# Picking 36 of 128 columns with a selection matrix, in place of a full transpose, behind the rotary attention

## The chip, the cores and the metric

The kernel runs on one core of a Trainium2 chip. The metric is the device time in microseconds (us), as the median of three runs. A core has five engines that run at the same time and wait for each other through semaphores: TensorE (PE; its weight loads are shown apart as PEld), VectorE (DVE), ScalarE (ACT), GpSimd (POOL) and SyncE (SP), which here only starts DMA transfers. TensorE multiplies a stationary operand, loaded into the array first, with a moving operand, and writes to the accumulator memory (PSUM, 8 banks of 512 fp32 words in each of 128 partitions). `nc.tensor.matmul(out, a, b)` computes aᵀb with a stationary; `nc.tensor.transpose(out, a, identity)` gives aᵀ and is one instruction with the same two operands.

## The reference

The program is four layers of attention and feed-forward, each `x = x + layernorm(f(layernorm(x)))`, over x of 8 batches x 512 tokens x 128 channels. The change touches the fourth attention (L3):

```
qkv = x @ Wqkv.T + bqkv            # 3 x 16 heads x 8 channels
q, k = rope(q), rope(k)
attn = softmax(q @ k.T / sqrt(8))  # per batch and head, 512 x 512
out = attn @ v                     # per head 512 x 8
return out.transpose(...).reshape(b, t, 128) @ Wout.T + bout
```

## The kernel before

`attention_layer` serves the first layer (L0) and, with `rope` true, the fourth (L3). It works on 32 quads; a quad `i` is 4 heads (index g) of one batch. For each quad TensorE does five kinds of work:

- `max_tile` (line 720): 16 products of queries and keys, from which VectorE takes the row maxima (`take`, line 921, two heads' tiles at a time, 8 per quad), two quads ahead of their use.
- `turn_max` (line 727): turns the split maxima; ScalarE copies them (`rows`, line 840) and a DMA puts them beside the queries.
- `score_tile` (line 733): 16 products, keys down the partitions; ScalarE takes the exponential of each (line 836).
- `pv` (line 743): 16 products with the values, for each head on a group of 32 partitions of bank 6. Row 32g + r of the result is channel r of head g for r below 8, and row 32g + 8 is the sum of that head's exponentials. The other 23 rows of a group are copies of that sum, since the padding of the values is 1.
- `pick` (line 752), in L3 only: VectorE has copied bank 6 to `o_quad` (`out`, line 933). `pick` turns each of the four 128-column pieces of it, so that tokens lie down the partitions. VectorE then takes the reciprocal of the sums (line 950) and multiplies (line 952) into `c.o`.

The order is written out by hand. In quad `i` TensorE runs k = 0 to 3; in k = 1 it runs two score tiles, `pv`, two score tiles, `pick(i - 1)`, the two max tiles of that k, then `turn_max(i + 1)`. Max tiles and picks share a ring of two places (banks 0 and 1, banks 2 and 3), the class `Ring`: an item may be written when the item two places before it is taken. So the second max tile of k = 1 waits until line 952 has read the pick. Score tiles, turns and projections share a second ring of three banks, emptied by ScalarE. VectorE runs `out(i - 1)` in k = 0, `normalise(i - 1)` (lines 950 and 952) at the head of k = 1, then two takes, and ScalarE runs `rows(i + 1)` behind the exponentials of k = 1. For i of 30 and 31 there are no max tiles left; `pick(31)` stands alone at the end.

Of other lines the prediction names 705 (the projection of the values: fp32, 128 stationary and 128 moving columns), 2459 (the gate of the last layer, 4 fp32 products with 128 stationary columns and 1 moving column per batch), 2471 (an fp32 product of 512 moving columns) and 1430 (VectorE, a product of 128 contiguous PSUM words per partition). `RotaryTables` loads constants in the first stage, on SP's queue; that stage ends when SP's loads have landed and ScalarE has copied the turned weights (TensorE line 140).

Of the kernel before, what the change touches and what calls it, by code (L numbers as in the profile page):

```python
# [14 lines left out]
TPB = S // 128  # L15
HEADS, HD = 16, 8
# [4 lines left out]
class Core:  # L21


    def __init__(self, nc, ctx):
        self.nc, self.ctx, self.sems = nc, ctx, []
        self.arena = ctx.enter_context(nc.sbuf_tensor("arena", [128, 48 * 1024], F32))
        self.psum = ctx.enter_context(nc.psum_tensor("psum", [128, 8 * 512], F32))
        self.used = 0
        self.x = self.take(TILES * D).rearrange("p (t c) -> p t c", c=D)
        self.n = self.take(TILES * D).rearrange("p (t c) -> p t c", c=D)  # L30
        self.o = self.take(TILES * D).rearrange("p (t c) -> p t c", c=D)

        self.nT = self.take(B * (S + 2)).rearrange("p (b s) -> p b s", s=S + 2)
        self.stats = self.take(TILES * 6).rearrange("p (t k) -> p t k", k=6)
        self.mv = self.take(TILES * 2).rearrange("p (t k) -> p t k", k=2)
        self.rstd = self.take(TILES)
        self.var_eps = self.take(TILES)
        self.minus_half = self.take(TILES)
        self.ident = self.take(128)
        self.ident_bf = self.take(64).bitcast(BF16)  # L40
        self.ones = self.take(128)
        self.wT = self.take(16 * 128).rearrange("p (w c) -> p w c", c=128)
        self.base = self.used
        self.gated = self.bank(6)
# [11 lines left out]
    def sem(self, name):  # L56
        self.sems.append(self.nc.alloc_semaphore(name))
        return self.sems[-1]
# [336 lines left out]
def attention_layer(c, tag, w, scale, tables=None, reload=None):  # L395
# [5 lines left out]
    nc = c.nc  # L401
# [31 lines left out]
    def for_vector():  # L433
        for i in range(2):
            for m in range(8):
                yield "max", i, m
        for i in range(QUADS):
            for k in range(4):
                if rope and k == 1 and i >= 1:
                    yield "pick", i - 1  # L440
                if i + 2 < QUADS:
                    yield "max", i + 2, 2 * k
                    yield "max", i + 2, 2 * k + 1
        yield "pick", LAST

    acts = Ring([c.bank(4), c.bank(5), c.bank(7)], for_scalar())
    maxes = Ring([c.bank(0, 2), c.bank(2, 2)], for_vector())
# [26 lines left out]
    ordered, q_pads, k_pads, k_ones = sem("ordered"), sem("q_pads"), sem("k_pads"), sem("k_ones")  # L474
    pool_step, dve_step = sem("pool_step"), sem("dve_step")
    if rope:
        qk_bias, v_bias, cos_t, sin_t = tables.qk_bias, tables.v_bias, tables.cos, tables.sin
        w_swap = c.take(256).rearrange("p (w c) -> p w c", w=2)
        other = both()
        swapped, summed, picked = sem("swapped"), sem("summed"), sem("picked")  # L480
        fetched = [sem(f"fetched{b}") for b in range(B)]
        of_o = LayerNorm(c, f"{tag}_norm_o")
# [7 lines left out]
    o_quad = c.take(2 * S).rearrange("p (s t) -> p s t", s=2)  # L490
# [3 lines left out]
    recip_done, o_done = sem("recip_done"), sem("o_done")  # L494
# [20 lines left out]
    with nc.Block() as block:  # L515
        @block.sync
        def _(sp):
# [38 lines left out]
            sp.wait_ge(k_pads, 2)  # L556
            sp.wait_ge(k_ones, 1)
            load(0)
            load(1)
            store(1, 0)  # L560
            store(1, 1)
            load(2)
            load(3)
            max_rows(0)
# [114 lines left out]
        def _(pe):  # L679
# [67 lines left out]
            def pick(i):  # L747

                pe.wait_ge(out_taken, i + 1)
                pe.wait_ge(max_taken, maxes.room(("pick", i)))  # L750
                for t in range(4):
                    last = nc.tensor.transpose(maxes.bank(("pick", i))[:, 128 * t:128 * t + 128],
                                               o_quad[:, i % 2, 128 * t:128 * t + 128], c.ident)
                last.then_inc(max_made, 1)

            pe.wait_ge(ordered, 1)
# [44 lines left out]
            if rope:  # L801
                pick(LAST)
# [76 lines left out]
        def _(dve):  # L879
# [55 lines left out]
            def normalise(i):  # L935

                b, s = divmod(i, TPB)
                if by_tokens:
                    dve.wait_ge(out_taken, i + 1)
                    o = o_quad[:, i % 2, :].rearrange("p (j r) -> p j r", r=32)  # L940
                    nc.vector.reciprocal(recip[:, i % 2, :], o[:, :, HD]).then_inc(recip_done, 1)
                    dve.wait_ge(recip_done, i + 1)
                    nc.vector.tensor_tensor(c.o[:, i, :].rearrange("p (j d) -> p j d", d=HD), o[:, :, 0:HD],
                                            recip[:, i % 2, :].unsqueeze(2).to_broadcast([128, HEADS, HD]),
                                            ALU.mult).then_inc(o_done, 1)
                else:
                    dve.wait_ge(max_made, maxes.count(("pick", i)))
                    o = maxes.bank(("pick", i))[:, 0:512].rearrange("p (t g r) -> p t g r", t=TPB, g=4)
                    r = recip[:, i % 2, :].rearrange("p (t g) -> p t g", t=4)
                    nc.vector.reciprocal(r, o[:, :, :, HD]).then_inc(recip_done, 1)  # L950
                    dve.wait_ge(recip_done, i + 1)
                    nc.vector.tensor_tensor(c.o[:, TPB * b:TPB * b + TPB, 32 * s:32 * s + 32].rearrange("p t (g d) -> p t g d", g=4),
                                            o[:, :, :, 0:HD],
                                            r.unsqueeze(3).to_broadcast([128, TPB, 4, HD]), ALU.mult).then_inc(max_taken, 1)
                    dve.wait_ge(max_taken, maxes.count(("pick", i)))
                    dve.sem_inc(o_done, 1)
# [21 lines left out]
            for i in range(QUADS):  # L978
                r, b = i % TPB, i // TPB + AHEAD + 1
                for k in range(4):  # L980
# [11 lines left out]
                    if b < B and (r, k) == (3, 2):  # L992
                        x_spread(b)
            out(LAST)
            normalise(LAST)


# [1345 lines left out]
class MixtureInputs:  # L2343
# [9 lines left out]
    def load(self, eng, d, signal):  # L2353
        eng.dma_start(self.w_switch, d["L1_ffn_w_switch"]).then_inc(signal, 16)
        eng.dma_start(self.w_choice, d["choice_gate"]).then_inc(signal, 16)
        eng.dma_start(self.wu, d["L3_ffn_Wu"]).then_inc(signal, 16)
        eng.dma_start(self.bu, d["L3_ffn_bu"].partition_broadcast(128)).then_inc(signal, 16)
        eng.dma_start(self.below, d["expert_below"]).then_inc(signal, 16)
        eng.dma_start(self.share, d["expert_share"]).then_inc(signal, 16)
        eng.dma_start(self.b2, d["L3_ffn_b2"].rearrange("e c -> (e c)").partition_broadcast(128)).then_inc(signal, 16)  # L2360
        eng.dma_start(self.b1[0:MIX * CHUNKS, :], d["L3_ffn_b1"].rearrange("e (k p) -> (e k) p", p=128)).then_inc(signal, 16)
# [270 lines left out]
def shape_constants():  # L2632

    import numpy as np
    half = HD // 2
    freq = (1.0 / np.float32(10000.0) ** (np.arange(0, HD, 2, dtype=np.float32) / np.float32(HD))).astype(np.float32)
    angle = np.outer(np.arange(S, dtype=np.float32), freq)
    row = np.arange(128)
    width = row // 4 % HD
    sign = np.where(width < half, -1.0, 1.0).astype(np.float32)  # L2640
    number = (np.arange(4)[None, :] - row[:, None]) % 4 + 1
    return {"rope_cos": np.cos(angle).astype(np.float32).T[width % half].copy(),
            "rope_sin": (np.sin(angle).astype(np.float32).T[width % half] * sign[:, None]).astype(np.float32),
            "expert_below": np.where(number == 1, -1.0, number - 1.0).astype(np.float32),
            "expert_share": (1.0 / number).astype(np.float32)}

# [10 lines left out]
class RotaryTables:  # L2657


    def __init__(self, c):  # L2660
        self.qk_bias = c.take(4)
        self.v_bias = c.take(D)
        self.cos, self.sin = c.take(S), c.take(S)
        self.loads = 4

    def load(self, eng, d, signal):
        eng.dma_start(self.qk_bias, d["qk_bias"]).then_inc(signal, 16)
        eng.dma_start(self.v_bias, d["L3_attn_bqkv"][2 * D:3 * D].partition_broadcast(128)).then_inc(signal, 16)
        eng.dma_start(self.cos, d["rope_cos"]).then_inc(signal, 16)
        eng.dma_start(self.sin, d["rope_sin"]).then_inc(signal, 16)  # L2670


def rotary_attention(c, d, tables, reload):

    attention_layer(c, "L3", W_QKV3, float(HD) ** -0.5, tables, reload)
    c.end_stage()
    c.free_work()
    project_heads(c, d)


def reshaped_attention(c):

    attention_layer(c, "L0", W_Q0, 1.0)
# [47 lines left out]
```

## Time and profile before

| | |
|---|---|
| median of 3 runs | 2190.15 us (2188.14 to 2192.21) |
| profiled execution, own time | 2190.15 us |
| its span, first to last instruction | 2188.4 us |
| TensorE busy | 1584.7 us (72%) |
| VectorE busy | 1256.0 us (57%) |
| ScalarE busy | 1079.2 us (49%) |
| GpSimd busy | 818.4 us (37%) |
| rotary attention, first to last pick | 1501 to 1912 us |

Busy time is summed over stages with different limits, so what an edit is worth is read in its own stage. Times in rows are microseconds from the start of the span; "mean" and the min/median/max of one instruction are nanoseconds. Matmuls overlap in the array: the distance from one start to the next says what one costs in a stream, its length says how late its result is. A row of the timeline merges neighbouring instructions of one line, xN is their count, and its length runs from the first start to the last end.

### The profile page before, as it was taken

How to read it: one execution, taken by the hardware profiler on the slowest of the kernel's cores; microseconds unless marked ns; L12 is line 12 of the kernel's file. 1: busy time of each engine (PE TensorE's matmuls, PEld its weight loads, DVE VectorE, ACT ScalarE, POOL GpSimd, SP SyncE). 2: the span in 40 equal slices, each digit the busy share in tenths (PEclk: the TensorE clock that was granted, in tenths of full speed). 3: DMA queues.
4: the chain of work that ended last, by engine and by line, in shares of the span. 5: the costliest groups of instructions: out<-in, count | busy, mean ns of one | idle time of the engine just before them, and what ended most of it. 6: DMA issues, size and time to landing. Idle time of an engine off the chain costs nothing. (4 is left out here: it accounts for less than half of the span.)

```text
span 2188.4 us, 25553 instructions
## 1 busy us (share of the span) xinstructions
PE 1584.7 (72%) x8294; PEld 812.2 (37%) x8294; DVE 1256.0 (57%) x2743; ACT 1079.2 (49%) x2160; POOL 818.4 (37%) x1482
## 2 busy tenths in 40 slices
PE   2799999963498850615530149358999999879998
PEld 1133333312365640504430036212333333257776
DVE  3688888856534230154468812176888878535443
ACT  1377777755333330246650013126777777645554
POOL 3455455325433335170061775543444431012111
PEclk8699999995755555856755569758999999989999
DMA  3221222100000021100003112311111111010000
GB/s 97 72 66 63 68 67 66 48 1 1 1 1 0 1 75 58 30 7 1 0 2 117 39 38 22 57 66 45 59 59 59 59 59 56 13 40 11 6 10 15
DMA packets 84952, 85.16 MB, mean 39 GB/s; under 512 B 35926, under 2 KB 67520, under 8 KB 84692
## 3 DMA queue, kind: packets, MB, share of 16 engines
q1 hardware_dynamic: 74900, 76.42, 10.7%
q0 software_dynamic: 7680, 6.06, 1.8%
q8 instruction: 67, 1.10, 0.2%
q10 hardware_dynamic: 2240, 1.05, 0.2%
q14 instruction: 65, 0.53, 0.1%
HBM read 59.76 MB, written 25.17 MB: 39 GB/s over the span
## 5 line engine op out<-in xcount | busy, mean ns | idle before, releaser
L921 DVE TENSOR_REDUCE arena<-psum 128x2 f32<-128x1024 f32 x512 | 602.1, 1218 | 131.9 <-PE psum L720 127.2
L836 ACT ACTIVATE arena<-psum 128x512 f32<-128x512 f32 x1024 | 553.6, 595 | 143.1 <-PE psum L733 134.1
L733 PE MATMUL psum<-arena 99*128 99x512 bf16 x1024 | 313.5, 388 | 16.4 <-DMA arena<-arena 11.8
L720 PE MATMUL psum<-arena 72*128 72x512 bf16 x1024 | 287.3, 397 | 40.8 <-POOL arena L622 18.5
L743 PE MATMUL psum<-arena 128*32 128x512 f32 x2048 | 275.3, 610 | 3.1 <-ACT arena L836 1.9
L733 PEld LDWEIGHTS psum<-arena 99*128 99x128 bf16 x1024 | 74.8, 98 | 295.5 <-ACT arena L836 224.6
L720 PEld LDWEIGHTS psum<-arena 72*128 72x128 bf16 x1024 | 95.8, 99 | 184.7 <-DVE arena L921 28.6
L2406 ACT ACTIVATE arena<-arena 128x128 f32<-128x128 f32 x252 | 102.4, 481 | 103.1 <-POOL arena L2394 103.1
L2389 POOL TENSOR_SCALAR arena<-arena 128x4 f32<-128x4 f32 x80 | 22.2, 277 | 304.3 <-DVE arena L2383 299.5
L631 POOL TENSOR_TENSOR arena<-arena 128x16 bf16<-128x16 f32 x64 | 13.8, 216 | 307.1 <-DVE arena L921 215.3
L344 ACT ACTIVATE arena<-arena 128x128 f32<-128x128 f32 x192 | 76.7, 480 | 96.3 <-POOL arena L260 70.9
L622 POOL COPY arena<-arena 72x1024 f32<-72x1024 f32 x64 | 64.9, 1041 | 154.7 <-PE psum L733 130.3
L2519 ACT ACTIVATE arena<-psum,arena 128x512 f32<-128x512 f32 x128 | 84.3, 682 | 77.3 <-PE psum L2471 75.2
L2483 PEld LDWEIGHTS psum<-arena 128*128 128x128 f32 x1024 | 118.1, 192 | 8.2 <-issue 8.2
L2483 PE MATMUL psum<-arena 128*128 128x128 f32 x1024 | 119.9, 275 | 0.0
L2471 PE MATMUL psum<-arena 128*128 128x512 f32 x256 | 116.8, 599 | 0.0
L332 PE MATMUL psum<-arena 128*128 128x128 f32 x96 | 26.7, 434 | 116.6 <-ACT arena L344 116.6
L2604 DVE SCALAR_TENSOR_TENSOR arena<-psum,arena 128x128 f32<-128x128 f32 x128 | 36.0, 344 | 126.9 <-PE psum L2483 126.2
L2380 DVE BATCH_NORM_STATS2 arena<-arena 128x6 f32<-128x128 f32 x320 | 69.1, 278 | 66.1 <-DMA arena<-ec_result 21.8
L2245 ACT ACTIVATE arena<-psum,arena 128x512 f32<-128x512 f32 x8 | 6.2, 777 | 183.3 <-issue 144.9
L2392 POOL TENSOR_TENSOR arena<-arena 128x4 f32<-128x4 f32 x80 | 83.2, 1040 | 6.7
L743 PEld LDWEIGHTS psum<-arena 128*32 128x32 f32 x2048 | 40.3, 108 | 109.6 <-ACT arena L836 60.5
(436 smaller groups left out, 2623.5 us busy)
## 6 DMA issues: line engine op xcount, KB each, us to landing
arena<-L_q_parts SPq DMA_DIRECT2D x192, 96.0 KB
arena<-L_k_parts SPq DMA_DIRECT2D x192, 96.0 KB
L_q_parts<-arena SPq DMA_DIRECT2D x16, 384.0 KB, 3.3
L_k_parts<-arena SPq DMA_DIRECT2D x16, 384.0 KB, 3.3
arena<-in_L_ffn_w SPq DMA_DIRECT2D x1, 2048.0 KB
ec_result<-arena SPq DMA_DIRECT2D x1, 2048.0 KB
arena<-in_L_ffn_fc2s SPq DMA_DIRECT2D x1, 2048.0 KB, 16.4
ec_normed<-arena SPq DMA_DIRECT2D x1, 2048.0 KB
```

The lines of the kernel that those rows point to most:

```text
L344: nc.scalar.activation(dst[:, t, :], src[:, t, :], ACT.Identity, bias=f.shift[:, t:t + 1], scale=f.scale[:, t:t + 1]).then_inc(signal, 1)
L720: last = nc.tensor.matmul(bank[:, 512 * h:512 * h + 512], columns(q9[0:QK_ROWS], i, m // 2, 128 * (2 * (m % 2) + h), 128), columns(k9[0:QK ...
L733: nc.tensor.matmul(acts.bank(name), columns(k9[0:ROWS], i, g, 128 * k, 128), columns(q9[0:ROWS], i, g, 0, 512), start=True, stop=True).the ...
L743: last = nc.tensor.matmul(out_bank[32 * g:32 * g + 32, :], v32[:, i % 2, g, k, :], prob[:, k % 2, g, :], start=(k == 0), stop=(k == 3))
L836: nc.scalar.activation(prob[:, k % 2, g, :], acts.bank(name), ACT.Exp, scale=scale).then_inc(act_taken, 1)
L921: nc.vector.tensor_reduce(neg_max[:, i % 2, 2 * m:2 * m + 2], maxes.bank(("max", i, m)).rearrange("p (h t) -> p h t", h=2), axis=AX.X, op= ...
L2380: self.nc.vector.bn_stats(self.stats[:, t, :], src[:, t, :]).then_inc(self.stats_done, 1)
L2392: self.nc.gpsimd.tensor_tensor(self.scale[:, at], self.var_eps[:, at], self.minus_half[:, 0:TPB], ALU.pow).then_inc(self.scale_done, 1)
L2406: self.nc.scalar.activation(dst[:, t, :], src[:, t, :], ACT.Identity, bias=self.shift[:, t:t + 1], scale=self.scale[:, t:t + 1]).then_inc( ...
L2471: nc.tensor.matmul(c.bank(k), w1[:, e, 128 * k:128 * k + 128], c.nT[:, b, 1:S + 1], start=True, stop=True).then_inc(h_made, 1)
L2483: last = nc.tensor.matmul(c.bank(4 + g % 2)[:, 128 * t:128 * t + 128], hT[:, g % 2, k, 128 * t:128 * t + 128], w2[:, e, k, :], start=(k == ...
L2519: nc.scalar.activation(hT[:, g % 2, k, :], c.bank(k), ACT.Relu, bias=b1T[:, CHUNKS * e + k:CHUNKS * e + k + 1]).then_inc(h_done, 1)
```

## The change

A constant matrix `select` of 128 x 36 is built beside the tables of the rotation, and loaded with them by one more DMA (128 rows of 144 bytes). Column 8g + r picks row 32g + r (channel r of head g), column 32 + g picks row 32g + 8 (its sum). `pick` multiplies each piece of `o_quad` (stationary, as before) with `select` by a plain fp32 matmul, where it transposed it with the identity: 36 output columns where there were 128, written side by side. VectorE reads the sums as 4 adjacent words and the channels as 32 adjacent words per tile, where it stepped over 128; the count of elements is the same. Constants behind `select` move up by 36 words in the on-chip memory.

```
-                    last = nc.tensor.transpose(maxes.bank(("pick", i))[:, 128 * t:128 * t + 128],
-                                               o_quad[:, i % 2, 128 * t:128 * t + 128], c.ident)
+                    last = nc.tensor.matmul(maxes.bank(("pick", i))[:, 36 * t:36 * t + 36], o_quad[:, i % 2, 128 * t:128 * t + 128],
+                                            select, start=True, stop=True)
...
-                    o = maxes.bank(("pick", i))[:, 0:512].rearrange("p (t g r) -> p t g r", t=TPB, g=4)
+                    o = maxes.bank(("pick", i))[:, 0:144].rearrange("p (t r) -> p t r", r=36)
...
-                    nc.vector.reciprocal(r, o[:, :, :, HD]).then_inc(recip_done, 1)
+                    nc.vector.reciprocal(r, o[:, :, 32:36]).then_inc(recip_done, 1)
...
-                                            o[:, :, :, 0:HD],
+                                            o[:, :, 0:32].rearrange("p t (g d) -> p t g d", g=4),
...
+    select = np.zeros((128, 36), np.float32)
+    for g in range(4):
+        for r in range(HD):
+            select[32 * g + r, HD * g + r] = 1.0
+        select[32 * g + HD, 4 * HD + g] = 1.0
...
-        self.loads = 4
+        self.select = c.take(36)
+        self.loads = 5
...
+        eng.dma_start(self.select, d["select_rows"]).then_inc(signal, 16)
```

TensorE's order in k = 1 of a quad, before (-) and after (+); a row gives the line, the output's shape and the number of calls:

```order
 L743 MATMUL psum<-arena 32x512 x4
 L733 MATMUL psum<-arena 128x512 x2
-L752 MATMUL psum<-arena 128x128 x4
+L752 MATMUL psum<-arena 128x36 x4
 L720 MATMUL psum<-arena 128x512 x4
 L727 MATMUL psum<-arena 48x128
```

Nothing changes place. The pick still stands between the last two score tiles and the max tiles of k = 1 (four calls of line 720), with the turn behind them. Calls are counted here, and one call may be more than one instruction in the trace.

At the very end of the stage TensorE has:

```order
 L733 MATMUL psum<-arena 128x512 x2
 L743 MATMUL psum<-arena 32x512 x4
-L752 MATMUL psum<-arena 128x128 x4
+L752 MATMUL psum<-arena 128x36 x4
 L515 UNCONDITIONAL_BRANCH
 L2302 UNCONDITIONAL_BRANCH
```

Here too only the form of the four calls is another; nothing of TensorE's stands behind them in this stage.

## Rows read from the trace of the kernel before

**Rows 1.** all instructions of line 752: ns min/median/max, first and last start
```profile
L752 PE MATMUL psum<-arena x128: 270/272/330, 1501.3 to 1912.3; 128*128 128x128 f32 x128
```

**Rows 2.** page, TensorE clock granted in 40 slices, tenths of full speed
```profile
PEclk8699999995755555856755569758999999989999
```

**Rows 3.** PE, PEld, DVE, ACT, POOL busy in a window; then clock, DMA
```profile
1500.00:1900.00 400.00, 391.04 (x2162) 130.02 (x2165) 318.72 (x398) 299.63 (x583) 141.65 (x295) 1.00 0.15 55
```

**Rows 4.** one pick and what follows, in order of time: start, length, engine, line
```profile
1640.11 0.58 PEld L752 LDWEIGHTS psum<-arena 128*128 128x128 f32 x4
...
1640.33 0.60 PE L752 MATMUL psum<-arena 128*128 128x128 f32 x4
...
1640.77 0.60 PE L720 MATMUL psum<-arena 72*128 72x512 bf16 x2
1640.97 0.26 DVE L950 RECIPROCAL arena<-psum 128x16 f32<-128x16 f32 x1 [0.48 <-PE psum L752]
1641.26 0.29 DVE L952 TENSOR_TENSOR arena<-psum,arena 128x128 f32<-128x128 f32 x1
...
1641.61 0.11 PEld L720 LDWEIGHTS psum<-arena 72*128 72x128 bf16 x2 [0.74 <-DVE arena L952]
1641.61 0.61 PE L720 MATMUL psum<-arena 72*128 72x512 bf16 x2 [0.24 <-DVE arena L952]
...
1642.15 0.24 PE L727 MATMUL psum<-arena 128*48 128x128 bf16 x1
...
1642.42 0.27 ACT L840 ACTIVATE arena<-psum 48x128 bf16<-48x128 bf16 x1 [1.02 <-PE psum L727]
```

**Rows 5.** waits in 1500 to 1915 us: total us, times, longest
```profile
ACT arena L840 <- PE psum L727: 29.7, 29, 1.0
...
PEld psum L720 <- DVE arena L952: 21.3, 29, 0.7
DVE arena L950 <- PE psum L752: 18.9, 32, 2.8
...
PE psum L720 <- DVE arena L952: 7.1, 29, 0.2
```

**Rows 6.** all instructions of line 2459 on TensorE
```profile
L2459 PE MATMUL psum<-arena x64: 165/250/374, 1941.6 to 2150.3; 128*128 128x1 f32 x64
```

**Rows 7.** all weight loads of line 705
```profile
L705 PEld LDWEIGHTS psum<-arena x128: 188/192/337, 30.8 to 1813.5; 128*128 128x128 f32 x128
```

**Rows 8.** TensorE in order of time around the value projection of line 705
```profile
1648.01 1.05 PE L705 MATMUL psum<-arena 128*128 128x128 f32 x8
...
1648.90 0.60 PE L733 MATMUL psum<-arena 99*128 99x512 bf16 x2
```

**Rows 9.** TensorE in order of time around the gate of line 2459
```profile
1969.95 3.60 PE L2471 MATMUL psum<-arena 128*128 128x512 f32 x8
1973.38 0.95 PE L2459 MATMUL psum<-arena 128*128 128x1 f32 x8
1974.19 3.82 PE L2483 MATMUL psum<-arena 128*128 128x128 f32 x32
```

**Rows 10.** order of time, end of the stage
```profile
1903.76 2.07 ACT L836 ACTIVATE arena<-psum 128x512 f32<-128x512 f32 x4 [0.50 <-PE psum L733]
...
1911.91 0.66 PE L752 MATMUL psum<-arena 128*128 128x128 f32 x4 [0.82 <-DVE arena L933]
1912.60 0.26 DVE L950 RECIPROCAL arena<-psum 128x16 f32<-128x16 f32 x1 [0.75 <-PE psum L752]
```

**Rows 11.** VectorE groups by line and form: busy, mean ns
```profile
L952 DVE TENSOR_TENSOR arena<-psum,arena 128x128 f32<-128x128 f32 x32 | 9.3, 291 | 1.1
...
L1430 DVE TENSOR_TENSOR arena<-psum,arena 128x128 f32<-128x128 f32 x8 | 2.3, 292 | 45.5 <-PE psum L1213 45.5
```

**Rows 12.** order of time, start of the program
```profile
12.13 0.43 SPq L2361 DMA_DIRECT2D arena<-in_L_ffn_b  x1
...
16.33 3.68 PE L140 MATMUL psum<-arena 128*128 128x128 f32 x16 [16.33 <-DMA arena<-in_L_attn_Wout]
```

More of the change, by code:

```diff
@@ L476, in attention_layer @@
     if rope:
-        qk_bias, v_bias, cos_t, sin_t = tables.qk_bias, tables.v_bias, tables.cos, tables.sin
+        qk_bias, v_bias, cos_t, sin_t, select = tables.qk_bias, tables.v_bias, tables.cos, tables.sin, tables.select
         w_swap = c.take(256).rearrange("p (w c) -> p w c", w=2)
@@ L2643, in shape_constants @@
             "rope_sin": (np.sin(angle).astype(np.float32).T[width % half] * sign[:, None]).astype(np.float32),
+            "select_rows": select,
             "expert_below": np.where(number == 1, -1.0, number - 1.0).astype(np.float32),
```

## The prediction, on record before the changed kernel ran

> **What bounds the kernel now.** I read first the clock in slices, then the busy times of the stage, then the timeline of one quad, and last the waits. The picks run from 1501 to 1912 us [rows 1]. In that stretch, slices 29 to 35 of the clock row, the clock is granted in full [rows 2], and over 1500 to 1900 us TensorE shows 391 us busy of 400, VectorE 319, ScalarE 300, GpSimd 142 [rows 3]. That puts TensorE first, but its busy time includes the tails of matmuls, so it is no proof. The timeline of one pick settles it [rows 4]. The reader should follow five starts: the pick at 1640.33, the first two max-tile matmuls at 1640.77, the reciprocal at 1640.97, the product at 1641.26, the next two max-tile matmuls at 1641.61. So TensorE does not simply run on behind a pick. It waits for the product to hand back the two banks (0.24 us of idle, weight load 0.74). Behind that come the turn at 1642.15, and ScalarE's copy of it, which had been idle for 1.02 us. All three engines thus hang on the end of the pick at this place: VectorE waits for it (0.48 us), TensorE waits for VectorE, ScalarE waits for TensorE. The waits say that this is so in every quad and not in this one alone: ScalarE waits for the turn 29 times, 29.7 us in all and 1.0 at the longest; TensorE's weight load waits for the product 29 times, 21.3 us, its matmuls 29 times, 7.1 us [rows 5].
>
> **The pick, before.** Each of the 128 instructions of line 752 takes 270 to 330 ns, median 272 [rows 1], and 32 picks make four each: a transpose is one instruction. In the stream four of them cost 1640.77 - 1640.33 = 0.44 us, or 0.11 each, and the last result is there 0.60 us after the first start [rows 4].
>
> **The pick, after.** It is an fp32 matmul, no transpose. The order counts four calls; the trace shows what a call becomes. Line 2459 makes 4 calls per batch, 32 in all, and the trace has 64 instructions [rows 6]; line 705 makes 64 calls in its two layers, and has 128 weight loads [rows 7]. Both are fp32 with a full 128 x 128 stationary operand. So a pick becomes 8 weight loads and 8 matmuls. What eight cost at full clock is bounded by two rows, one at either side of 36 columns:
> - 128 moving columns, line 705: 1648.90 - 1648.01 = 0.89 us, result after 1.05 [rows 8].
> - 1 moving column, line 2459: 1974.19 - 1973.38 = 0.81 us, result after 0.95 [rows 9].
>
> From 128 columns to 1 the cost hardly falls: what is paid for is the reload of 128 stationary columns, and cutting the moving side to 36 saves almost nothing. The change cuts the side that is cheap, and doubles the number of loads. The new pick costs 0.81 to 0.89 in the stream, 0.37 to 0.45 more than 0.44; its result is later by 0.35 (0.95 - 0.60) to 0.45 (1.05 - 0.60). I take 0.41 for both, the middle of the stream's difference.
>
> A rule of the Trainium skill speaks the other way. The page "TensorE: Matmul & The Clock Gate", section "Back-to-back issue gap", gives about 60 cycles at 2.4 GHz for any matmul of 1 to 64 columns and 134 for 128. By it eight matmuls of 36 columns would take an estimated 0.2 us, and the pick would get cheaper. The row of line 2459 disagrees: one column costs 0.81 / 8 = 0.10 us per instruction there [rows 9]. The same page, section "LDWEIGHTS (loading the stationary operand)", makes the load go by its columns, an estimated 107 ns for 128; with that the trace agrees (0.10 to 0.11).
>
> **What of it lies on the path.** Picks 0 to 28 are followed by max tiles, 29 in number. There TensorE's next pair of max-tile matmuls starts 0.41 later, the reciprocal and the product 0.41 later, so the pair behind the product too, and with it the turn, ScalarE's copy and the takes. Nothing at that place had been waiting for something else than the pick or TensorE's stream, so nothing swallows it. The 0.24 us wait for the product stays as it was: both of its sides move. 29 x 0.41 = 11.9 us. Queued behind the longer pick on TensorE are exactly those max tiles and the turn; behind the product on VectorE stand two takes, which wait for these max tiles anyway.
>
> Picks 29 and 30 have no max tiles behind them. There ScalarE runs four exponentials without a gap, 2.07 us, after waiting 0.50 for TensorE [rows 10], so part of the delay is hidden. Each costs 0 to 0.45; I take 0.15 each, nearer to hidden, as ScalarE has 2.07 us of work in hand: 0.3 us. The last pick stands alone: 0.66 us from its first start, and the reciprocal right behind it at 1912.60 [rows 10]. It pays the whole difference, 0.35 to 0.45; I take 0.4.
>
> **VectorE's reads.** They have the same counts of elements, but adjacent words. Line 952 takes 291 ns with steps in PSUM; line 1430, the same operation on 128 adjacent PSUM words, 292 [rows 11]. I count nothing. For the reciprocal (0.26 us in [rows 4]) no such pair exists; I bound both instructions together by the 0.03 us between 0.26 and 0.29, up or down, 29 x 0.03 = 0.9 us either way.
>
> **The added load.** It stands on SP's queue in the first stage. SP's last issue there starts at 12.13 and takes 0.43 [rows 12]; one more moves it by about as much, to some 13.0. TensorE starts on the weights at 16.33 and works 3.68 us before the stage can end [rows 12]. That hides it; if the 18 KB shared the transfer engines badly with those weights, the price is at most one such issue, 0.4 us, and not below 0. I take 0. The 36 words by which later buffers move change no size of a transfer; 0.
>
> **Sum.** 11.9 + 0.3 + 0.4 = 12.6 us. The profiled execution took 2190.15 us itself, 1.75 more than its span of 2188.4, and it is equal to the median, so no correction: 2190.15 + 12.6 = 2202.8 us. The bounds: least 29 x 0.35 + 0 + 0.35 - 0.9 = 9.6, most 29 x 0.45 + 0.9 + 0.45 + 0.9 + 0.4 = 15.7, or 2199.8 to 2205.9.
>
> **Rivals.**
> - *Fewer columns win.* If a matmul's cost here went by its moving columns, then from 3.60 us for eight of 512 columns (line 2471, [rows 9]) one of 36 would cost 0.45 x 36 / 512 = 0.03, eight 0.25, and a pick would be 0.19 us shorter: 29 x 0.19 = 5.5 faster, about 2184.6. It decides as soon as a weight load hides behind the matmul before it. For it: 512 columns do cost 0.45 and 128 about 0.11. Against it: 1 column costs 0.10, on the same kind of operand and near full clock (slice 37 of [rows 2]). Chance 0.04. The table of gaps in the Trainium skill, named above, says much the same as this rival.
> - *The delay is swallowed.* If something other than the pick set the pace of a quad, the 0.41 would go into a gap: 2190.2 to 2191. For it: VectorE has 81 us of idle time in 400 and ScalarE 100. Against it: both wait for TensorE at this very place [rows 5], so both are moved along. Chance 0.05.
> - *Loads that don't overlap.* A load of 128 fp32 columns is 188 to 337 ns long by itself, median 192 [rows 7]. Were the eight loads run one after another with their matmuls (median 250 ns, [rows 6]), each pair would take 0.19 + 0.25 = 0.44 us and a pick 8 x 0.44 = 3.5, 3.1 more: 29 x 3.1 = +90 us, 2280. Against it: rows of eight at 0.81 and 0.89. Chance 0.02.
> - *Half on the path.* The delay counts in the quads, but VectorE or ScalarE makes part of it good further on in those quads where a layer norm or a projection lies beside them: 4 to 9 us, 2194 to 2199. Nothing in the rows shows it. Chance 0.07.
>
> **How the numbers follow.** The forecast has 0.82, at 2202.8, with its own range of 2199.8 to 2205.9. The runs of before lie 2 us to either side of their median. Widened by part of that, the range is 2198.5 to 2206.5. It leaves out most of the rivals. A measurement of this kernel tells a change from none at about 0.2%, 4.4 us; 12.6 us is 0.58%. Slower by more than that: the forecast, the unhidden loads and half of the half case, 0.88. Within: the swallowed case and the other half, 0.08. Faster: 0.04.
>
> **What would show it.** Line 752 with 256 instructions of about 250 to 275 ns and as many weight loads; 0.81 to 0.89 us from the first matmul of a pick to the next max tile; the reciprocal 1.05 us behind that first matmul, not 0.64 [rows 4]; VectorE's wait for the pick grown by 0.4; a pick-to-pick distance 0.4 longer in every quad; lines 950 and 952 at 258 and 291 ns; the first stage as before. It would be wrong if line 752 showed 128 instructions, or the second pair of max-tile matmuls came less than 0.3 us later behind the pick, or the quads were no longer.

## The result

The changed kernel takes 2201.91 us (2201.46 to 2204.19, 4 runs), the kernel before 2189.34 us (2188.14 to 2192.21, 4 runs, shared). The medians differ by 12.6 us, where 12.6 us had been forecast on a base of 2190.15. The ratio, which takes in 21 runs of the changed kernel, is 1.0063, with a 95% interval of 1.0051 to 1.0076: slower by 13.8 us, 11.2 to 16.6. That the medians of these few runs meet the sum to the tenth is luck, and so in part is the sum: below, one of its terms comes out smaller and another larger.

### The profile page after: what moved, and what is told of

Its sections match the earlier page's. It is cut to its first block and busy times, and to the rows that moved or that the text cites. A ratio compares the mean times of both kernels' runs of the same rounds, so it can differ in the third digit from the quotient of the medians.

```text
span 2190.9 us, 25810 instructions
## 1 busy us (share of the span) xinstructions
PE 1588.8 (73%) x8422; PEld 824.9 (38%) x8422; DVE 1256.8 (57%) x2743; ACT 1080.2 (49%) x2160; POOL 819.4 (37%) x1482
## 3 DMA queue, kind: packets, MB, share of 16 engines
q8 instruction: 68, 1.11, 0.2%
q10 hardware_dynamic: 2240, 1.05, 0.2%
## 5 line engine op out<-in xcount | busy, mean ns | idle before, releaser
L631 POOL TENSOR_TENSOR arena<-arena 128x16 bf16<-128x16 f32 x64 | 13.8, 216 | 317.6 <-DVE arena L921 223.3
```

## The profile after

TensorE, VectorE and ScalarE around one pick, in order of time, as in [rows 4]:

```profile
1646.18 1.08 PEld L752 LDWEIGHTS psum<-arena 128*128 128x128 f32 x8
1646.40 0.98 PE L752 MATMUL psum<-arena 128*128 128x36 f32 x8
...
1647.21 0.60 PE L720 MATMUL psum<-arena 72*128 72x512 bf16 x2
1647.42 0.26 DVE L950 RECIPROCAL arena<-psum 128x16 f32<-128x16 f32 x1 [0.86 <-PE psum L752]
1647.71 0.29 DVE L952 TENSOR_TENSOR arena<-psum,arena 128x128 f32<-128x128 f32 x1
1648.06 0.11 PEld L720 LDWEIGHTS psum<-arena 72*128 72x128 bf16 x2 [0.74 <-DVE arena L952]
1648.06 0.60 PE L720 MATMUL psum<-arena 72*128 72x512 bf16 x2 [0.24 <-DVE arena L952]
...
1648.60 0.24 PE L727 MATMUL psum<-arena 128*48 128x128 bf16 x1
1648.87 0.27 ACT L840 ACTIVATE arena<-psum 48x128 bf16<-48x128 bf16 x1 [1.40 <-PE psum L727]
```

Measure each row from the pick's first matmul. The next max tiles come after 0.81 us (0.44 before), the reciprocal after 1.02 (0.64), the second pair of max tiles after 1.66 (1.28), the turn after 2.20 (1.82). Everything behind the pick moved by the same 0.37 to 0.38. VectorE's wait grew from 0.48 to 0.86 and ScalarE's from 1.02 to 1.40, by the same amount: both were already waiting here, so nothing could swallow it. TensorE's own wait for line 952 is 0.24 as before.

All instructions of line 752, then the waits of the stage, which answer to [rows 1] and [rows 5]:

```profile
L752 PEld LDWEIGHTS psum<-arena x256: 186/192/333, 1489.7 to 1913.1; 128*128 128x128 f32 x128
L752 PE MATMUL psum<-arena x256: 196/279/407, 1489.9 to 1913.1; 128*128 128x36 f32 x128
```

```profile
ACT arena L840 <- PE psum L727: 39.2, 28, 1.4
...
DVE arena L950 <- PE psum L752: 31.0, 31, 3.2
PEld psum L720 <- DVE arena L952: 20.6, 28, 0.7
```

128 matmuls have become 256. The window of 1500 to 1915 us cuts off one pick here (28 and 31 waits, 29 and 32 before), since the stage starts earlier in this execution: the picks begin at 1490 us, not 1501, and the expert layer ahead of them was shorter in this one profile. The span, 2190.9 us, is thus no measure of the change; the 21 times are all above 2201. The length of the stage is: from the first pick's start to the last one's 410.6 us before and 421.9 after. Of this the first 29 distances make up 391.86 and 402.75: 10.89 more, 0.376 each. (The distances from first to last pick in the expectations below, 411.0 and 423.2, run to the last instruction of the last pick, as in [rows 1], and so take in what the clock does to that pick.)

## Experiments

The runs of one kernel scatter by up to 11 us (before: 2187.7 to 2199.1 over all comparisons). In the profiles the scatter lies outside this stage: over the twelve of them the first pick starts anywhere from 1490 to 1507 us, and 276.5 to 279.2 us pass from the last pick's start to the end. So for each kernel both are given: the ratio of the times, and the sum of the first 29 pick-to-pick distances in its profile, which repeats to 0.02 us (the changed kernel: 402.75 and 402.73). Distances are the starts of line 752 read from the timeline; the experiments were run in three groups, each with its own runs of the kernel before.

**The changed kernel again.**

> The changed kernel once more, for a second profile: in its first one the layer before the rotary attention was some 11 us shorter than in all other profiles, which the times do not show. Theory (that was this one execution's): the picks start near 1500 to 1507 us and span 423.2 minus or plus 1 us, each quad 0.38 longer than before. Rival (the change also shortens that layer): the picks start near 1490 again.

2204.44 us, ratio 1.0057 (1.0035 to 1.0080). The picks start at 1501 us and the 29 distances sum to 402.73. From first to last pick it is 421.8 from start to start, and 422.6 by the count of the expectation, which had 423.2, give or take 1. The short layer was that one execution's; the span here is 2201.6 us. The theory holds.

**The load alone.** From the kernel before, with the new constant and its transfer but the old pick:

```
+        self.select = c.take(36)
+        self.loads = 5
+        eng.dma_start(self.select, d["select_rows"]).then_inc(signal, 16)
```

> The kernel before, with the selection matrix loaded in the first stage and later buffers moved up by 36 words, but not used: the pick is the transposes of before. Theory: nothing, within 1 us, and TensorE's first instruction of the program at most 0.4 us later; distance from first to last pick 411. Rival: the load or the moved buffers are part of the 12.6 us, 2 us or more.

2194.18 us, ratio 1.0000 (0.9988 to 1.0012); 391.85 against 391.86 in the kernel before. TensorE's first instruction starts at 16.46, where it was 16.33 [rows 12]; in the two profiles of the changed kernel it starts at 16.57 and 16.86. That is about half a microsecond at most, and the load costs nothing that can be measured in the times.

**Columns.** A plain matmul with the full identity:

```
-                    last = nc.tensor.transpose(maxes.bank(("pick", i))[:, 128 * t:128 * t + 128],
-                                               o_quad[:, i % 2, 128 * t:128 * t + 128], c.ident)
+                    last = nc.tensor.matmul(maxes.bank(("pick", i))[:, 128 * t:128 * t + 128],
+                                            o_quad[:, i % 2, 128 * t:128 * t + 128], c.ident, start=True, stop=True)
```

> The kernel before, with the pick as a plain fp32 matmul against the 128-column identity, 128 columns written, all else as before. Theory (loads): eight weight loads set the cost and the moving columns are free; 0.89 us in the stream and the result after 1.05, as in line 705, so 0.44 more than the transposes for 29 picks, some 13.5 us in all: about 2203, at most 2 us above the changed kernel. Rival (columns): if the 36 columns save something, this kernel pays for 128: two passes of 92 more columns at 2.4 GHz are 0.08 us per instruction, 0.6 per pick, some 18 us above the changed kernel, 2220.

2209.42 us, ratio 1.0068 (1.0047 to 1.0089), an interval that overlaps the change's. The distances sum to 405.02: 13.16 more than before, 0.454 each, and 2.3 more than the changed kernel, where 2 at most had been expected. One pick:

```profile
1563.91 1.05 PE L752 MATMUL psum<-arena 128*128 128x128 f32 x8
...
1564.80 0.60 PE L720 MATMUL psum<-arena 72*128 72x512 bf16 x2
```

0.89 us in the stream, as line 705 had it. So 92 columns fewer save 0.08 us of a pick, and going from a transpose to a matmul costs 0.45. The rival's 18 us on top did not come. One caution: eight fp32 matmuls of 512 columns take 3.60 us [rows 9], 0.45 each, so 128 columns would by themselves take an estimated 0.11, as much as the reload does. With 128 columns the two limits cannot be told apart; with 36 (an estimated 0.03) they can.

**Number.** The transposes of before, each made twice:

```
-                for t in range(4):
+                for t in [0, 1, 2, 3, 0, 1, 2, 3]:
```

> The kernel before, with each of the four transposes of a pick made twice, to the same place: eight loads and eight matmuls in transpose form. Theory (loads): what counts is that there are eight; 8 x 0.11 = 0.88 us in the stream, +0.44 x 29 + 0.75 = about +13.5, 2203. Rival (fp32 passes): the cost lies in fp32 arithmetic that a transpose does not do, so that eight transposes are cheaper than eight halves of fp32 matmuls: under 0.7 us for eight, and less than +8 us.

2202.18 us, ratio 1.0046 (1.0028 to 1.0064); 404.47, 12.61 more than before, 0.435 each. One pick:

```profile
1571.53 1.04 PE L752 MATMUL psum<-arena 128*128 128x128 f32 x8
1572.30 0.21 PEld L720 LDWEIGHTS psum<-arena 72*128 72x128 bf16 x2
...
1572.40 0.60 PE L720 MATMUL psum<-arena 72*128 72x512 bf16 x2
```

0.87 us. Eight transposes cost what eight halves of fp32 matmuls cost, to 0.02. Of the 0.454 us by which the matmul with the identity was dearer, 0.435 goes with the number: a transpose is cheap here for being one instruction where a matmul is two. Whether each of the eight is held up by its load or by its 128 moving columns this run does not say, by the caution above.

**Width of the loads.** The changed kernel with stationary pieces of 64 columns; the upper half of each tile's tokens is not picked:

```
-                    ... maxes.bank(("pick", i))[:, 36 * t:36 * t + 36], o_quad[:, i % 2, 128 * t:128 * t + 128],
+                    ... maxes.bank(("pick", i))[0:64, 36 * t:36 * t + 36], o_quad[:, i % 2, 128 * t:128 * t + 64],
```

> The changed kernel, with each stationary piece of a pick cut from 128 to 64 columns; the upper 64 tokens of each tile are left out of the pick, all other work stays. Still eight loads and eight matmuls of 36 moving columns. Theory (loads by their columns): a load of half the columns takes half of 0.11, so eight take about 0.45, as the four transposes did, and the distance from first to last pick is 411 to 414 us, as in the kernel before (411.0), not 423.2. Rival (cost per instruction): about 0.1 us is a floor for any pair of load and matmul, and the distance stays at 421 to 423.

2198.35 us, ratio 1.0014 (1.0005 to 1.0024); 396.05, 6.7 less than the changed kernel, and 4.19 more than before, 0.144 per pick. From first to last pick it is 415.2 by the count of the expectation, 1.2 beyond the theory's range and far from the rival's. The rows say why not all of the cost is gone:

```profile
1559.31 0.61 PE L733 MATMUL psum<-arena 99*128 99x512 bf16 x2
1559.85 0.54 PEld L752 LDWEIGHTS psum<-arena 128*64 128x64 f32 x8 [0.43 <-issue]
1559.85 0.66 PE L752 MATMUL psum<-arena 128*64 128x36 f32 x8
...
1560.54 0.26 DVE L950 RECIPROCAL arena<-psum 128x16 f32<-128x16 f32 x1 [0.40 <-PE psum L752]
```

A load of 64 columns is 0.138 us long (median), eight end after 0.54, so they start (0.54 - 0.138) / 7 = 0.057 apart: about half of 0.11, as expected. As the moving columns are the same 36, this is the experiment that ties the cost to the load. But the first load no longer starts ahead, under the score tile: pick and load start together, 0.54 behind the score tiles, where the full-width pick starts 0.44 to 0.45 behind them. That is 0.10 of the 0.144; the rest is the result, for which VectorE reads 0.69 us behind the pick's start and not 0.64 [rows 4].

**Half the bytes.** The kernel before with the output rounded to bf16 in VectorE's copy (its precision is lower by that) and the pick as four bf16 matmuls:

```
-                    nc.vector.tensor_copy(o_quad[:, i % 2, :], out_bank).then_inc(out_taken, 1)
+                    nc.vector.tensor_copy(o_half[:, i % 2, :], out_bank).then_inc(out_taken, 1)
...
+                                            o_half[:, i % 2, 128 * t:128 * t + 128], c.ident_bf, start=True, stop=True)
```

> The kernel before, with the accumulated output rounded to bf16 as VectorE copies it, and the pick as four plain bf16 matmuls against the bf16 identity, 128 columns; the rounding lowers the precision of the layer's output. Theory (number and width of the loads): four loads at the bf16 pace (0.10 for two, as line 720's) take 0.22 us in the stream and the result is there after some 0.42, so 0.18 to 0.22 less than the transposes for 29 picks and a little at the end: 5 to 6.5 us faster than before, picks spanning about 405. Rival (transposing is what is cheap): plain matmuls cost more than transposes whatever the type: no gain or a loss.

2188.88 us, ratio 0.9971 (0.9962 to 0.9981): 6.4 us faster. The distances sum to 385.62, 6.24 less than before, 0.215 each; the picks span 404.3. One pick (lines count one higher in this kernel):

```profile
1572.33 0.39 PE L753 MATMUL psum<-arena 128*128 128x128 bf16 x4
...
1572.56 0.60 PE L721 MATMUL psum<-arena 72*128 72x512 bf16 x2
1572.76 0.26 DVE L951 RECIPROCAL arena<-psum 128x16 f32<-128x16 f32 x1 [0.27 <-PE psum L753]
```

The stream pays 0.23 us, and the reciprocal comes after 0.43, 0.21 earlier than before. VectorE's copy takes 0.69 us in either type. Four plain bf16 matmuls are thus cheaper than four fp32 transposes, so a plain matmul is not dear as such. What limits each of them, 0.057 us, is not shown: two bf16 score tiles of 512 columns take 0.44 us, by which 128 columns take an estimated 0.055, the same again.

**Place, with the old pick.** TensorE's order in k = 1:

```
+                    if rope and k == 1 and i >= 1:
+                        pick(i - 1)
                     score_tile(i, k, 2)
                     score_tile(i, k, 3)
-                    if rope and k == 1 and i >= 1:
-                        pick(i - 1)
```

> The kernel before, with the pick moved ahead of the last two score tiles of k = 1; TensorE runs pick, score, score, max tiles. Theory (both paths): the second pair of max tiles now comes 0.44 + 0.44 + 0.44 = 1.32 us after the pick's first start, and VectorE's product is done at 1.24, so the wait of 0.40 us between its start and the stream's end is gone: 29 x 0.39 = 11 us faster, about 2178. Rival (other engines): once this wait is gone ScalarE or VectorE sets the pace of the quad, and less than 4 us are won, 2185 or more.

2180.74 us (2180.24 to 2183.01), ratio 0.9949 (0.9935 to 0.9962). 381.21, 10.65 less than before, 0.367 each, where the theory had 0.39. One pick:

```profile
1569.81 0.42 PEld L752 LDWEIGHTS psum<-arena 128*128 128x128 f32 x4 [0.84 <-issue]
1569.81 0.66 PE L752 MATMUL psum<-arena 128*128 128x128 f32 x4
...
1570.30 0.60 PE L733 MATMUL psum<-arena 99*128 99x512 bf16 x2
1570.50 0.26 DVE L950 RECIPROCAL arena<-psum 128x16 f32<-128x16 f32 x1
...
1570.74 1.03 PE L720 MATMUL psum<-arena 72*128 72x512 bf16 x4
1570.80 0.29 DVE L952 TENSOR_TENSOR arena<-psum,arena 128x128 f32<-128x128 f32 x1
```

The four max-tile matmuls stand in one row of x4, with no wait for line 952 between them. The pick itself costs 0.05 more in the stream (0.49), since its first load does not hide behind `pv`. In the last two quads, which have no max tiles to gain on, the early pick costs time: ScalarE's exponentials wait 0.98 us for the score tiles behind it, where they waited 0.50, and each of these quads is 0.48 longer. About 9.7 us are left of the 10.65. This kernel beats both.

**Place, with the new pick.** The same edit on the changed kernel:

> The changed kernel with the same move of the pick. Theory (both paths): the wait for VectorE goes here too (second pair after 0.81 + 0.44 + 0.44 = 1.69, product done at 1.64), but the longer pick stays in TensorE's stream, 0.37 x 31 = 11.5 us above the kernel before with the same move: about 2190. Rival (result only): the change cost time only because the pick's result was late for VectorE and the two max tiles; two score tiles now cover it, and the kernel comes within 3 us of the moved kernel before.

2194.62 us, ratio 1.0006 (0.9994 to 1.0019). 393.23, which is 12.02 more than the moved kernel before, 0.41 each, and 1.4 more than the kernel before. One pick:

```profile
1575.49 1.08 PE L752 MATMUL psum<-arena 128*128 128x36 f32 x8
...
1576.40 0.60 PE L733 MATMUL psum<-arena 99*128 99x512 bf16 x2
```

The time is above the 2190 that had been expected, and the rival falls: with the result covered by two score tiles, the longer stream (0.91 against 0.49) still shows in full. In the change both ways of counting gave the same number, so the change alone could not tell them apart.

**Place and the turn.** `turn_max` ahead of the two max tiles too, from the moved kernel before:

```
+                    if k == 1 and i < LAST:
+                        turn_max(i + 1)
                     if i + 2 < QUADS:
...
-                    if k == 1 and i < LAST:
-                        turn_max(i + 1)
```

> The kernel before with the pick ahead of the last two score tiles of k = 1 (early_before), and the turn of the maxima ahead of the two max tiles as well. Theory (TensorE's stream is the path once the wait for VectorE is gone): ScalarE's idle time ahead of line 840 only moves elsewhere; within 2 us of the kernel with the early pick, picks spanning 401 to 403. Rival (ScalarE is the next bound): the earlier turn lets it run ahead, 3 us or more faster than that kernel.

2184.04 us, ratio 0.9953 (0.9936 to 0.9969); 380.97 against 381.21. The time is 3.3 us above that of the moved kernel, where 2 had been allowed, but in its group the kernel before ran 2.6 us longer too, and the ratios agree. ScalarE's wait there is not on the path once TensorE's stream is.

**Place, one step too far.** The pick ahead of `pv`, from the kernel before:

```
+                    if rope and k == 1 and i >= 1:
+                        pick(i - 1)
                     if k >= 1:
                         pv(i, k - 1)
```

> The kernel before, with the pick moved ahead of pv in k = 1, behind the first two score tiles. Theory (TensorE's stream): the first weight load of the pick hides behind a bf16 score tile again, so the pick costs 0.44 and not 0.49 in the stream, and nothing waits for VectorE: 29 x 0.05 = 1.5 us faster than with the pick behind pv; picks spanning about 400 instead of 401.3, some 11 us faster than before, 2179 to 2181. Rival (ScalarE next): its exponentials wait for the scores that now come 0.44 later behind the pick, and the gain shrinks to under 8 us.

2204.48 us, ratio 1.0053 (1.0036 to 1.0069): slower than before, where 11 us faster was expected. The distances sum to 401.05, 9.2 more than before and 19.8, or 0.68 each, more than with the pick behind `pv`. Both readings had it faster, and both missed the ring:

```profile
1574.84 2.36 DVE L921 TENSOR_REDUCE arena<-psum 128x2 f32<-128x1024 f32 x2 [0.25 <-PE psum L720]
...
1575.07 0.60 PE L733 MATMUL psum<-arena 99*128 99x512 bf16 x2
...
1576.18 0.42 PEld L752 LDWEIGHTS psum<-arena 128*128 128x128 f32 x4 [1.01 <-issue]
1576.21 0.63 PE L752 MATMUL psum<-arena 128*128 128x128 f32 x4 [0.54 <-DVE arena L921]
...
1576.77 1.06 PE L743 MATMUL psum<-arena 128*32 128x512 f32 x8
...
1578.19 1.09 ACT L836 ACTIVATE arena<-psum 128x512 f32<-128x512 f32 x2 [1.56 <-PE psum L733]
```

The pick needs the place of the max tile two before it, which VectorE takes first among the two takes of 1574.84, at 1.2 us each; it is free only at about 1576.1. So the pick starts 1.14 us behind the first two score tiles, where `pv` starts 0.52 behind them without it (1876.19 and 1876.71 in the kernel before), and takes 0.56 of the stream where it took 0.49 behind `pv`. These 0.62 and 0.07 make up the 0.68, to 0.01; `pv`, the scores behind it and ScalarE with them are late by it. Placed behind `pv` (1.0 us of work), the pick finds its place free.

## Why the prediction was right, step by step

- *A pick becomes eight loads and eight matmuls.* Right: 256 instructions of line 752. They are 279 ns at the median, slightly over the 250 to 275 named.
- *0.81 to 0.89 in the stream, result after 0.95 to 1.05.* Right, and at the low end: 0.81 and 0.98. The middle that I took, 0.41, was too high: 0.376 was measured. With 1 column [rows 9] and 36 the stream costs the same, 128 cost 0.89. That reloads set it at 36 columns is shown by the moving columns, 92 of which change 0.08 us (ident), and by the width of a load, half of which halves the step (half). That their number counts is shown in transpose form (twice). The bf16 run agrees with the reading, and would agree with a limit by moving columns too.
- *All of it on the path, 29 times.* Right: every one of the first 29 distances grew by 0.36 to 0.38, those with projections beside them too. The term is 10.89 us, not 11.9.
- *Picks 29 and 30, 0.3 us.* Measured 0.17 and 0.22, together 0.39.
- *The last pick, 0.4 us.* Right at full clock, and left open to the clock, which the prediction did not count. Its eight matmuls take 1.79 us in the first profile, against 0.66 before [rows 10], and 1.08 in the second, at the granted clocks below. The 0.65 there is a mean over both levels: the clock is 1.00 (2.4 GHz) up to 1911.7 and 0.50 (1.2 GHz) from 1912.2 on. In the experiment with the load alone, the old pick's transposes took 1.11 at 0.63, again with 0.50 from 1915.2 on. The pick stands behind a wait in which TensorE does nothing for 0.8 us, and whether the clock falls during the pick differs from one execution to the next, with either pick. So the term is 0.42 with both at full clock, 0.68 with both at the fallen one, and up to 1.1 where only the new pick is caught.
- *VectorE's reads, nothing.* Right: lines 950 and 952 have medians of 258 and 291 ns, before and after.
- *The load, nothing.* Right (load).

In sum 10.9 + 0.4 + 0.4 to 1.1 = 11.7 to 12.4 us, beside 12.6 (medians) and 13.8 (ratio, 11.2 to 16.6) measured in the times. The spans of the second profile and of before show where such a difference can lie: 2201.6 - 2188.4 = 13.2 us, of which 0.1 is ahead of the first pick, 11.3 between first and last pick, and 1.8 behind the last pick's start. The last pick explains 0.4 of these 1.8. The kernel with the load alone, whose pick is the old one, is also 1.5 us longer than before in this last part (0.45 of it the last pick at the lower clock), so such differences come without the change too; what they are stays open.

The rival *fewer columns win* had the sign wrong in its premise: a load does not hide behind a short matmul. The table that the prediction names beside it, from the page "TensorE: Matmul & The Clock Gate" of the Trainium skill, section "Back-to-back issue gap", is given there for the isolated gap of a single matmul, and the section itself says that at small N this counts too little where each matmul has its own load. So it never spoke for this rival; the 0.10 us per pair measured here fits the section's own warning. *The delay is swallowed* and *half on the path* fall with the 29 equal distances. *Loads that don't overlap* falls with 0.81 for eight.

Granted clock (the third figure from the end) around the last pick, before, after, and in the second profile of after:

```profile
1911.00:1914.00 3.00, 0.75 (x8) 0.42 (x4) 1.24 (x3) 0.00 (x0) 0.00 (x0) 1.00 0.00 0
```

```profile
1911.00:1914.00 3.00, 1.79 (x8) 1.65 (x8) 1.07 (x3) 0.00 (x0) 0.00 (x0) 0.65 0.00 0
```

```profile
1922.00:1925.00 3.00, 1.56 (x16) 0.97 (x8) 1.24 (x3) 0.00 (x0) 0.00 (x0) 1.00 0.00 0
```

## What to carry to other kernels

With small fp32 operands on TensorE, count the pairs of weight load and matmul, and the stationary columns of each, before the moving columns, as long as these are 128 or fewer in fp32: here a transpose of 128 columns was one pair and a matmul of 36 columns two, and the narrower one cost 0.37 us more per group of four. Where an instruction's result goes round through another engine and back into the same stream, put independent work of the stream behind it: two score tiles behind the old pick were worth about 10 us, about as much as the choice of the instruction (11). And before moving it forward, look up which buffer it writes and who must have emptied it; one step further than that, the same move cost 9 us.

## What I had not expected of the hardware

The first load of a pick starts ahead of its matmul in some places and not in others. It does behind bf16 score tiles (0.22 us ahead, 1646.18 and 1646.40 above); it does not behind `pv`, whose matmuls run on groups of 32 columns (the old pick then costs 0.49 and not 0.44), nor behind the same score tiles when it has 64 columns and not 128 (both at 1559.85). Each time it is 0.05 to 0.10 us. The runs show where it happens and not why.
